# Projections of a graph network's first attention: score factors stored once and doubled by the loads, the first attention loads issued ahead of the meeting, 30 of 157 row sums placed behind the products

## The chip, the core and the metric

One core of a Trainium2 chip (trn2) runs the whole kernel. The metric is the device time of one execution in microseconds (us). The engines named below: TensorE (PE in the rows; PEld is its loading of weights), VectorE (DVE), ScalarE (ACT), GpSimd (POOL) and SyncE (SP), which here only issues DMAs. They run side by side and meet at semaphores.

## The reference, cut to what matters

Four layers of a graph network on 3125 nodes with 96 features and 100000 edges, sorted by destination. The change touches the first and, through the row sums, the last:

```python
h = relu(layernorm(x))
q = (h[src] @ qW).reshape(e, 4, 24);  k = (h[dst] @ kW).reshape(e, 4, 24);  v = (h[dst] @ vW)...
exp_s = exp(clip(einsum('ehd,ehd->eh', q, k), -10, 10))
w = exp_s / (segment_sum(exp_s, src)[src] + 1e-08)
x = x + h + segment_sum(w * v, src)
# layers 2 and 3: gated messages, neighbour sums
deg = segment_sum(ones, src);  dis = where(deg > 0, rsqrt(max(deg, 1)), 0)   # layer 4
```

## The kernel before

The kernel first builds CT, the matrix of edge counts between nodes, in SBUF (25 tiles of 128 rows, 3136 columns, float16). Everything later works on CT, and three meetings of all five engines (`meet`, L71) separate four stages: build, projections, attention, and propagation with the last layer.

**Projections.** The nodes are taken in seven blocks of 512 (the last has 64). For each block b TensorE turns the normalised features (`turn`, L868), multiplies them with the query and key weights (`products`, L896) and with the value weights (L902). The score factors must be more exact than float16, so each is kept as a high part (ScalarE, `highs`, L831) and a low part (VectorE, `low`, L783) in `K.QH[:, b % 2]`, two slots in turn. SP stores them (`proj_sync`, L675) to HBM buffers `qd` and `kd` of 4 x 24 rows for each of four heads: qd holds high, high, low, low and kd holds high, low, high, low, so that one product over 96 rows gives all four cross terms. Each part is stored twice through a broadcast, four transfers of 192 KB a block. `highs(b)` waits for the four stores of block b - 2 before it overwrites their slot. SP then waits for all stores, meets, and only then issues the first attention loads.

**Attention.** It runs over 175 iterations: seven blocks of source nodes b (512 columns in blocks 0 to 3, 384 in 4 and 5, 320 in 6), and for each 25 tiles t of destinations. In an iteration TensorE computes four scores (L1065) from Kb and Qb, ScalarE their exponentials (L1117), GpSimd clamps them (L978), TensorE turns the counts (L1054), VectorE weighs (L1136), and TensorE multiplies with the values (L1075), in that order per iteration: scores of it + 2, counts of it + 1, values of it - 1. SP issues K loads (L1012) into a ring of NK = 3 slots: the load for it + 3 waits for the scores of it. At t = 0 of blocks 1 to 5 it issues the Q load (L1005) of the next block, at t = 5 it waits for VectorE's sum of the block before and stores it (L1023), at t = 10 it loads the next x1 (L1018). All on the one queue of SP, in this order.

**Propagation.** TensorE works through seven groups of nodes: it turns and multiplies them (`linear`, L1281 and L1290), adds one eighth of the row sums of CT (`source_sums`, L1307, 157 matmuls of up to 500 columns into one bank) and starts the first product (L1299), while VectorE normalises and splits the groups (L1464 to L1516). After the last group VectorE reduces the bank to the source degrees (`degrees`, L1439).

The lines printed below are those of the kernel before.

Of the kernel before, what the change touches and what calls it, by code (L numbers as in the profile page):

```python
# [651 lines left out]
def proj_sync(q, K):  # L652
# [19 lines left out]
    def store(to, b, n, i):  # L672

        wb = width(b)
        q.dma_start(to.rearrange("r c h w -> (c h) r w")[:, :, 0:wb], bcast_out(K.QH[:, b % 2, n, i, 0:wb], 2, wb)  # L675
                    ).then_inc(S("q_out%d" % (b % 2)), 16)

    for b in range(7):
        q.wait_ge(S("q_low"), 2 * b + 1)
        for i in range(2):  # L680
            store(K.qd[b, 2 * i:2 * i + 2], b, 0, i)
        q.wait_ge(S("q_low"), 2 * b + 2)
        for i in range(2):
# [126 lines left out]
def proj_scalar(a, K):  # L810
# [47 lines left out]
def proj_tensor(t, K):  # L858
    S, bank = K.S, K.bank

    def turn(b):
# [5 lines left out]
        for i in range(tiles(b)):  # L867
            m = t.transpose(bank((0, 3)[b % 2])[0:96, 128 * i:128 * i + 128], K.hb[:, 4 * b + i, :], K.identf[:, :])  # L868
# [73 lines left out]
def alloc_attn(K, st):  # L942
# [5 lines left out]
    K.Qb = sb(st, "Qb", [96, 2, 4, 512], F16)  # L948
    K.Kb = sb(st, "Kb", [96, NK, 4, 128], F16)
# [17 lines left out]
def q_loaded(b):  # L967
    return 16 * sum(len(list(q_pieces(i))) for i in range(b % 2, b + 1, 2))
# [27 lines left out]

def attn_sync(q, K):
    S = K.S

    def q_load(b):  # L1000
        if b >= 2:
            q.wait_ge(S("scores"), 2 * (25 * (b - 2) + 24) + 2)
        for c, w in q_pieces(b):
            o = c - 128 * B0[b]
            q.dma_start(K.Qb[:, b % 2, :, o:o + w], K.qd[c // 512].rearrange("r c h w -> (r c) h w")[:, :, c % 512:c % 512 + w]  # L1005
                        ).then_inc(S("q_in%d" % (b % 2)), 16)

    def k_load(it):
        b, t, wb, na, r = dims(it)
        if it >= NK:  # L1010
            q.wait_ge(S("scores"), 2 * (it - NK) + 2)
        q.dma_start(K.Kb[:, it % NK, :, 0:r], K.kd[t // 4].rearrange("r c h w -> (r c) h w")[:, :, 128 * (t % 4):128 * (t % 4) + r]  # L1012
                    ).then_inc(S("k_in%d" % (it % NK)), 16)
# [30 lines left out]
def attn_tensor(p, K):  # L1044
# [13 lines left out]
    def score(it, k):  # L1058
# [3 lines left out]
        p.wait_ge(S("k_in%d" % (it % NK)), 16 * (it // NK + 1))  # L1062
# [114 lines left out]
SRC_W = 20  # L1177
SRC_N = (NP + SRC_W - 1) // SRC_W
# [95 lines left out]
def prop_tensor(p, K):  # L1274
# [29 lines left out]
    def source_sums(i):  # L1304
        for k in range(i * SRC_N // 8, (i + 1) * SRC_N // 8):
            w = min(SRC_W, NP - SRC_W * k)
            m = p.matmul(bank(FIRST - 1)[:, 0:NT * SRC_W].rearrange("p (a w) -> p a w", w=SRC_W)[:, :, 0:w], K.identb[:, :],  # L1307
                         K.CT[:, :, SRC_W * k:SRC_W * k + w], start=(k == 0), stop=(k == SRC_N - 1), skip_group_check=True)
# [120 lines left out]
def prop_vector(v, K):  # L1429
# [428 lines left out]
def gnn_kernel(nc, x, srcp, dstp, ewp, qW, kW, vW, Wv, bv, W2, b2, w2, bb2, w3, bb3, w4, bb4,  # L1858
               attn_w, attn_b, fus_w, fus_b, gamma, beta, out):
    with ExitStack() as ctx:  # L1860
# [10 lines left out]
        K.qd, K.kd = dram("qd", 7, 4, 24, 4, 512, dt=F16), dram("kd", 7, 4, 24, 4, 512, dt=F16)  # L1871
# [112 lines left out]
```

## Time and profile before

| | us |
|---|---|
| median of 3 runs (1189.02 to 1191.69) | 1190.76 |
| the profiled execution | 1189.85 |
| its span on the core | 1187.9 |
| busy TensorE, VectorE | 1017.8 (86%), 888.2 (75%) |
| busy ScalarE, GpSimd | 605.4 (51%), 488.9 (41%) |
| projections, from the first to the second meeting | 361 to 409.6 |
| attention, to the third meeting | 409.6 to 794.6 |

The span is what the profiled instructions cover; the time of an execution is 1.9 us longer. Times inside the profile count from the span's start. 77% of the chain that ended last is TensorE's.

### The profile page before, as it was taken

To read this page: it belongs to the slowest core of one execution; us is meant where nothing else is said; L and a number is where in the kernel's file an instruction comes from. 1 tells how busy PE (TensorE), PEld (TensorE's weight loads), DVE (VectorE), ACT (ScalarE), POOL (GpSimd) and SP (SyncE) were. 2 spreads that over 40 slices of the span, in tenths; PEclk is the share of its full clock that TensorE was granted. 3 is DMA by queue.
4 is the path that set the end of the run, shared out by engine and by line. 5 is a ranking of instruction groups with operands and counts; after the bars stand their busy time and mean duration, and the time that the engine had idled before them with its cause. 6 is when DMAs were issued, how large, how long until landed. Compare 5 with 4: busy or idle time off the path is not lost.

```text
span 1187.9 us, 23158 instructions
## 1 busy us (share of the span) xinstructions
PE 1017.8 (86%) x8352; PEld 623.3 (52%) x8352; DVE 888.2 (75%) x1338; ACT 605.4 (51%) x816; POOL 488.9 (41%) x518
## 2 busy tenths in 40 slices
PE   3887777778879599999999999987997899998983
PEld 2554555445545322222233333334587799998873
DVE  8768887888665489999999999978656464533576
ACT  7556556555653399898989898851000000000321
POOL 8545433532100089999999999840000000000000
PEclk9879888887788889999999999988999799999996
DMA  0010000000001811212122222220000000010201
GB/s 8 27 42 10 5 6 5 6 9 6 15 1 48 247 41 43 68 42 69 43 66 45 70 58 66 67 69 1 1 28 34 25 35 10 2 40 8 84 17 41
DMA packets 98906, 44.79 MB, mean 38 GB/s; under 512 B 85196, under 2 KB 96716, under 8 KB 98672
## 3 DMA queue, kind: packets, MB, share of 16 engines
q1 hardware_dynamic: 97104, 41.58, 13.2%
q0 software_dynamic: 1696, 1.74, 0.5%
q8 instruction: 74, 1.21, 0.4%
q14 instruction: 32, 0.26, 0.1%
HBM read 30.73 MB, written 12.56 MB: 36 GB/s over the span
## 4 chain that ended last, share of the span: by engine, by line
PE 77%; issue 8%; DVE 7%; ACT 3%; POOL 3%; DMA 2%; SPq 1%; DVEq 0%; ACTq 0%; POOLq 0%
PE PS L1299 17%; PE PS L1065 12%; PE PS L553 11%; PE PS L1075 11%; PE PS L557 8%; PE PS L1739 3%; PE PS L1307 3%; PE PS L1054 3%; ACT Eb L1117 2%; PE PS L1290 1%; POOL Eb L978 1%; DVE Eb L1136 1%; PE PS L878 1%; PE PS L1746 1%; PE PS L1729 1%
## 5 line engine op out<-in xcount | busy, mean ns | idle before, releaser
L1136 DVE TENSOR_TENSOR Eb<-Eb,PS 128x2048 f32<-128x2048 f32 (+4 forms) x175 | 342.1, 2014 | 20.8 <-POOL Eb L978 10.6
L1117 ACT ACTIVATE Eb<-PS,small 128x1024 f32<-128x1024 f32 (+4 forms) x350 | 333.6, 1004 | 37.2 <-PE PS L1065 32.3
L978 POOL TENSOR_SCALAR Eb<-Eb 128x1024 f32<-128x1024 f32 (+4 forms) x350 | 318.9, 935 | 79.1 <-ACT Eb L1117 75.3
L593 ACT ACTIVATE CT<-PS 128x500 f32 x313 | 183.8, 587 | 143.4 <-PE PS L557 135.6
L553 PE MATMUL PS<-mov,oneS 128*128 128x100 f16 x1565 | 185.3, 232 | 76.8 <-issue 71.7
L553 PEld LDWEIGHTS PS<-mov,oneS 128*128 128x128 f16 x1565 | 147.1, 108 | 159.6 <-issue 114.6
L1299 PE MATMUL PS<-hs,CT 128*128 128x192 f16 (+1 forms) x2500 | 213.4, 247 | 3.6 <-DVE SG L1540 1.6
L1299 PEld LDWEIGHTS PS<-hs,CT 128*128 128x128 f16 (+1 forms) x2500 | 208.0, 99 | 7.3 <-DVE SG L1540 2.3
L1065 PE MATMUL PS<-Qb,Kb 96*128 96x512 f16 (+3 forms) x700 | 180.8, 362 | 14.5 <-DMA Kb<-kd 10.2
L435 DVE TENSOR_TENSOR oneS<-iotaX,KL 128x2560 f16<-128x2560 int16 x80 | 120.5, 1506 | 72.2 <-PE PS L557 69.6
L1075 PE MATMUL PS<-Eb,V 128*25 128x512 f32 (+3 forms) x1400 | 166.9, 549 | 0.8 <-DVE Eb L1136 0.8
L1065 PEld LDWEIGHTS PS<-Qb,Kb 96*128 96x128 f16 (+1 forms) x700 | 42.4, 98 | 199.6 <-ACT Eb L1117 185.7
L557 PE MATMUL PS<-CT,identb 128*128 x313 | 144.2, 461 | 0.9 <-ACT CT L593 0.8
L435 DVE TENSOR_TENSOR mov<-iotaM,KL 128x2000 f16<-128x2000 int16 x80 | 98.0, 1225 | 0.0
L217 POOL TENSOR_SCALAR key<-hi 120x128 f32<-120x128 int32 x14 | 8.8, 628 | 173.2 <-DVE hi L444 173.1
L1054 PEld LDWEIGHTS PS<-identb,CT 128*128 128x128 f16 (+1 forms) x625 | 49.6, 99 | 44.4 <-DVE Eb L1136 8.0
L1420 ACT ACTIVATE hs<-PS 96x96 f32<-96x96 f32 x9 | 2.2, 247 | 138.3 <-PE PS L1331 138.3
L1054 PE MATMUL PS<-identb,CT 128*128 128x128 f16 (+1 forms) x625 | 66.7, 220 | 4.4 <-DVE Eb L1136 4.4
L1540 DVE TENSOR_REDUCE SG<-PS 128x96 f32<-128x192 f32 (+1 forms) x75 | 24.8, 353 | 60.7 <-PE PS L1299 60.3
L1739 PE MATMUL PS<-hs,CT 97*128 97x297 f32 (+1 forms) x200 | 44.4, 366 | 0.0
L1307 PE MATMUL PS<-CT,identb 128*128 128x500 f16 (+1 forms) x157 | 39.1, 407 | 3.3 <-SPq L71 3.3
L1739 PEld LDWEIGHTS PS<-hs,CT 97*128 97x128 f32 (+1 forms) x200 | 36.2, 196 | 6.9 <-issue 0.6
(273 smaller groups left out, 892.4 us busy)
## 6 DMA issues: line engine op xcount, KB each, us to landing
Kb<-kd SPq DMA_DIRECT2D x168, 96.0 KB, 2.3
qd<-QH SPq DMA_DIRECT2D x12, 192.0 KB, 3.0
kd<-QH SPq DMA_DIRECT2D x12, 192.0 KB, 3.2
hs<-t_d SPq DMA_DIRECT2D x12, 192.0 KB, 2.6
Qb<-qd SPq DMA_DIRECT2D x4, 384.0 KB, 3.6
CT<-x_d SPq DMA_DIRECT2D x1, 1200.0 KB, 9.2
x_d<-B SPq DMA_DIRECT2D x6, 192.0 KB, 1.8
t_d<-A SPq DMA_DIRECT2D x6, 192.0 KB, 1.8
```

What stands on the lines that cost most here:

```text
L435: return v.tensor_tensor(out.rearrange("p e (c two) -> p e c two", two=2), v_in, k_in, ALU.is_equal)
L553: t.matmul(to, K.oneS[:, s % DEEP, o + k, :], K.mov[:, s % DEEP, o + k, :].rearrange("p (a w) -> p a w", a=25), start=(k == 0), stop=False ...
L557: t.matmul(ps, K.identb[:, :], K.CT[:, :, bass.ds(vals[0], GI * W)], start=False, stop=True, skip_group_check=True).then_inc(S("counted"), 1)
L593: a.activation(K.CT[:, :, bass.ds(words[g % 4][0], GI * W)], K.bank(g % 4)[:, 0:25 * GI * W].rearrange("p (a c) -> p a c", a=25), ACT.Copy ...
L978: g.tensor_scalar(e, e, EHI, ELO, ALU.min, ALU.max).then_inc(S("clamped"), 1)
L1054: m = p.transpose(K.cntv[it % 2][0:r, 128 * i:128 * i + w], K.CT[0:w, B0[b] + i, 128 * t:128 * t + r], K.identb[0:w, 0:w])
L1065: m = p.matmul(bank(h)[0:r, 0:wb], K.Kb[:, it % NK, h, 0:r], K.Qb[:, b % 2, h, 0:wb], start=True, stop=True)
L1075: m = p.matmul(bank(4)[32 * h:32 * h + 25, 0:wb], K.V[0:r, t, h, :], K.Eb[0:r, it % NE_, h, 0:wb], start=(t == 0), stop=(t == NT - 1), til ...
L1117: a.activation(e, ps, ACT.Exp, scale=K.unsc[0:r, :]).then_inc(S("score_exp"), 1)
L1136: v.tensor_tensor(e, e, cn, ALU.mult).then_inc(S("weighed"), 1)
L1299: m = p.matmul(bank(t % FIRST)[0:r, 0:w], K.CT[:, a, 128 * t:128 * t + r], hs[:, a, :, :].rearrange("p k d -> p (k d)"), start=(a == 0), s ...
L1739: m = p.matmul(ps[:, c:297], K.TT[0:r, s, 128 * k:128 * k + 128], K.GC[0:r, k, c:297], start=(k == 0), stop=(k == 3), skip_group_check=True)
```

## The change

- `qd` and `kd` hold two parts instead of four rows of parts, high and low once each: one store per factor and block, without the broadcast (14 stores instead of 28).
- The doubling moves to the loads. A Q load is four transfers of 24 partitions, each part read twice; a K load is two of 48 partitions, the same source twice.
- SP issues the loads of Q blocks 0 and 1 and of the first three K tiles before the second meeting, behind waits for the stores that they read. `Qb` and `Kb` are therefore allocated beside the projection buffers, and `hb` becomes a ring of 16 tiles with a wait for the turns of the block that used it.
- The first 30 of the 157 row-sum matmuls run after the last products, into bank 0; VectorE reduces them into `K.part`. The other 127 stay in the eight places between the groups of propagation, and `degrees` adds the two sums.

The diff, cut to its core:

```diff
@@ -607,12 +607,30 @@
+SRC_W = 20
+SRC_N = (NP + SRC_W - 1) // SRC_W
+EARLY = 30
+
+def row_sums(p, K, b, i, j):
+    for k in range(i, j):
+        w = min(SRC_W, NP - SRC_W * k)
+        m = p.matmul(K.bank(b)[:, 0:NT * SRC_W].rearrange("p (a w) -> p a w", w=SRC_W)[:, :, 0:w], K.identb[:, :],
+                     K.CT[:, :, SRC_W * k:SRC_W * k + w], start=(k in (0, EARLY)), stop=(k in (EARLY - 1, SRC_N - 1)),
+                     skip_group_check=True)
+    return m
+
+def add_rows(v, K, b, out):
+    return v.tensor_reduce(out, K.bank(b)[:, 0:NT * SRC_W].rearrange("p (a w) -> p a w", w=SRC_W), AX.X, ALU.add)
-    K.hb = sb(st, "hb", [128, NT, D], F32)
+    K.hb = sb(st, "hb", [128, 16, D], F32)
@@ -669,26 +687,29 @@
-        q.dma_start(to.rearrange("r c h w -> (c h) r w")[:, :, 0:wb], bcast_out(K.QH[:, b % 2, n, i, 0:wb], 2, wb)
+        q.dma_start(to.rearrange("i c h w -> (c h) i w")[:, :, 0:wb], K.QH[:, b % 2, n, :, 0:wb]
                     ).then_inc(S("q_out%d" % (b % 2)), 16)
 
     for b in range(7):
         q.wait_ge(S("q_low"), 2 * b + 1)
-        for i in range(2):
-            store(K.qd[b, 2 * i:2 * i + 2], b, 0, i)
+        store(K.qd[b], b, 0)
         q.wait_ge(S("q_low"), 2 * b + 2)
-        for i in range(2):
-            store(K.kd[b, i:4:2], b, 1, i)
+        store(K.kd[b], b, 1)
...
+    q.wait_ge(S("q_out0"), 32 * 3)
+    q_load(q, K, 0)
+    for it in range(NK):
+        k_load(q, K, it)
+    q.wait_ge(S("q_out1"), 32 * 3)
+    q_load(q, K, 1)
+    q.wait_ge(S("q_out0"), 32 * 4)
     q.wait_ge(S("x1_out"), 32)
-    q.wait_ge(S("q_out0"), 64 * 4)
-    q.wait_ge(S("q_out1"), 64 * 3)
@@ -719,11 +740,14 @@
+        if b >= 4:
+            v.wait_ge(S("h_turned"), b - 3)
@@ -802,6 +826,8 @@
+    v.wait_ge(S("src_part"), 1)
+    add_rows(v, K, 0, K.part).then_inc(step, own.up())
@@ -827,7 +853,7 @@
-                a.wait_ge(S("q_out%d" % (b % 2)), 64 * (b // 2))
+                a.wait_ge(S("q_out%d" % (b % 2)), 32 * (b // 2))
@@ -927,7 +953,9 @@
+    row_sums(t, K, 0, 0, EARLY).then_inc(S("src_part"), 1)
     t.wait_ge(S("v_made"), 7)
+    t.wait_ge(S("src_part"), 1)
@@ -994,23 +1020,29 @@
+def q_load(q, K, b):
+    S = K.S
+    if b >= 2:
+        q.wait_ge(S("scores"), 2 * (25 * (b - 2) + 24) + 2)
+    for c, w in q_pieces(b):
+        o = c - 128 * B0[b]
+        for r in range(4):
+            q.dma_start(K.Qb[24 * r:24 * r + 24, b % 2, :, o:o + w], K.qd[c // 512, r // 2, :, :, c % 512:c % 512 + w]
+                        ).then_inc(S("q_in%d" % (b % 2)), 16)
+
+def k_load(q, K, it):
+    S = K.S
+    b, t, wb, na, r = dims(it)
+    if it >= NK:
+        q.wait_ge(S("scores"), 2 * (it - NK) + 2)
+    kt = K.kd[t // 4].rearrange("i c h w -> (i c) h w")[:, :, 128 * (t % 4):128 * (t % 4) + r]
+    for i in range(2):
+        q.dma_start(K.Kb[48 * i:48 * i + 48, it % NK, :, 0:r], kt).then_inc(S("k_in%d" % (it % NK)), 16)
@@ -1023,16 +1055,12 @@
-    q_load(0)
-    for it in range(NK):
-        k_load(it)
-    q_load(1)
     x1_in(0)
@@ -1302,10 +1328,7 @@
+        m = row_sums(p, K, FIRST - 1, EARLY + i * (SRC_N - EARLY) // 8, EARLY + (i + 1) * (SRC_N - EARLY) // 8)
@@ -1436,9 +1459,10 @@
+        add_rows(v, K, FIRST - 1, K.degs).then_inc(S("src_kept"), 1)
         v.wait_ge(S("src_kept"), 1)
+        v.tensor_tensor(K.degs, K.degs, K.part, ALU.add).then_inc(step, own.up())
+        v.wait_ge(step, own.n)
@@ -1868,7 +1892,7 @@
-        K.qd, K.kd = dram("qd", 7, 4, 24, 4, 512, dt=F16), dram("kd", 7, 4, 24, 4, 512, dt=F16)
+        K.qd, K.kd = dram("qd", 7, 2, 24, 4, 512, dt=F16), dram("kd", 7, 2, 24, 4, 512, dt=F16)
```

What stands in a row on the engines now, in the three places that matter. On TensorE at the end of the projections (L896 and L922 are the factor products, L902 and L928 the value products, L1065 and L1093 the first scores), before:

```order
L902 MATMUL PS<-wv,hTb 128x96 x4
L868 MATMUL PS<-identf,hb 96x128
L896 MATMUL PS<-hTb,wqk 96x512 x2
L902 MATMUL PS<-wv,hTb 128x96 x4
L896 MATMUL PS<-hTb,wqk 96x64 x2
L902 MATMUL PS<-wv,hTb 64x96
L1065 MATMUL PS<-Qb,Kb 128x512 x8
```

and after the change:

```order
L928 MATMUL PS<-wv,hTb 128x96 x4
L894 MATMUL PS<-identf,hb 96x128
L922 MATMUL PS<-hTb,wqk 96x512 x2
L928 MATMUL PS<-wv,hTb 128x96 x4
L922 MATMUL PS<-hTb,wqk 96x64 x2
L928 MATMUL PS<-wv,hTb 64x96
L619 MATMUL PS<-CT,identb 128x500 x30
L1093 MATMUL PS<-Qb,Kb 128x512 x8
```

The row sums (L619) stand between the last value product and the meeting that precedes the first scores.

On SP in the same place, the stores of the last two blocks and the first loads; before, the meeting stands behind the last store:

```order
L688 DMA x_d<-X 128x1248
L675 DMA qd<-QH 96x2x512 x2
L675 DMA kd<-QH 96x2x512 x2
L675 DMA qd<-QH 96x2x64 x2
L675 DMA kd<-QH 96x2x64 x2
L1005 DMA Qb<-qd 96x2048
L1012 DMA Kb<-kd 96x4x128 x3
L1005 DMA Qb<-qd 96x2048
L1018 DMA xb<-x_d 128x384
```

and after the change, with the meeting behind the last of the 14 loads:

```order
L704 DMA x_d<-X 128x1248
L693 DMA qd<-QH 96x2x512
L693 DMA kd<-QH 96x2x512
L693 DMA qd<-QH 96x2x64
L693 DMA kd<-QH 96x2x64
L1030 DMA Qb<-qd 24x2048 x4
L1041 DMA Kb<-kd 48x4x128 x6
L1030 DMA Qb<-qd 24x2048 x4
L1050 DMA xb<-x_d 128x384
```

Eight stores have become four, five loads have become fourteen, and these have moved ahead of the meeting.

On SP at the start of attention block 4, where the two pieces of Q for block 5 are loaded between K loads; before:

```order
L1012 DMA Kb<-kd 96x4x64
L1012 DMA Kb<-kd 96x4x128 x4
L1005 DMA Qb<-qd 96x4x128
L1005 DMA Qb<-qd 96x4x256
L1012 DMA Kb<-kd 96x4x128 x5
```

and after the change:

```order
L1041 DMA Kb<-kd 48x4x64 x2
L1041 DMA Kb<-kd 48x4x128 x8
L1030 DMA Qb<-qd 24x4x128 x4
L1030 DMA Qb<-qd 24x4x256 x4
L1041 DMA Kb<-kd 48x4x128 x10
```

The K load behind the Q loads has eight issues ahead of it instead of two, and is itself two.

## Rows read from the trace of the kernel before

**Rows 1.** Chain of waits, 400 to 414 us: start, us, what.

```profile
401.11 3.27 DMA kd<-QH
...
407.98 1.60 DMA kd<-QH
...
410.02 3.50 DMA Kb<-kd
...
413.91 1.03 PE PS L1065 x2
```

**Rows 2.** Waits of ScalarE, 380 to 410 us: total us, times, longest.

```profile
ACT QH L831 <- DMA kd<-QH: 8.0, 5, 2.5
```

**Rows 3.** Timeline of TensorE, end of the products: start us, us, operation.

```profile
400.91 0.48 PE L896 MATMUL PS<-hTb,wqk 96*96 96x64 f32 x4
```

**Rows 4.** Timeline of ScalarE and VectorE, last block and the second meeting.

```profile
404.46 0.33 ACT L831 ACTIVATE QH<-PS 96x64 f16<-96x64 f32 x2 [1.21 <-DMA kd<-QH]
...
404.72 0.35 DVE L783 TENSOR_TENSOR QH<-PS,QH 96x64 f16<-96x64 f32 x2 [1.01 <-ACT QH L831]
...
410.91 0.08 DVE L1128 MEMSET rs<- 128x25 f32 x1
```

**Rows 5.** Windows: us, busy PE, PEld, DVE, ACT, POOL, then PEclk, DMA share, GB/s.

```profile
390.00:401.00 11.00, 10.47 (x57) 6.67 (x56) 7.42 (x19) 5.46 (x12) 0.00 (x0) 1.00 0.92 284
...
405.00:410.00 5.00, 0.00 (x0) 0.00 (x0) 0.30 (x2) 0.00 (x0) 0.00 (x0) 0.50 0.67 185
...
807.00:808.00 1.00, 0.00 (x0) 0.00 (x0) 0.97 (x5) 0.04 (x1) 0.00 (x0) 0.66 0.00 0
```

**Rows 6.** Timeline of SP: issues of K and Q loads in blocks 4 and 5.

```profile
650.95 0.54 SPq L1012 DMA_DIRECT2D Kb<-kd  x1
651.53 1.28 SPq L1005 DMA_DIRECT2D Qb<-qd  x2
...
665.89 1.86 SPq L1012 DMA_DIRECT2D Kb<-kd  x3
...
698.53 0.54 SPq L1012 DMA_DIRECT2D Kb<-kd  x1
```

**Rows 7.** Lines L675, L1005 and L1012: duration of an issue, ns min/median/max; landing.

```profile
L675 SPq DMA_DIRECT2D qd<-QH x14: 304/467/1352, 386.7 to 406.8; - x14
...
L1005 SPq DMA_DIRECT2D Qb<-qd x9: 315/617/618, 409.7 to 699.8; - x9
...
L1012 SPq DMA_DIRECT2D Kb<-kd x175: 540/541/659, 410.0 to 781.0; - x175
...
DMA to landing us min/median/max: 2.1/2.3/3.5
```

**Rows 8.** Timeline of TensorE: the starts of four scores in blocks 4 and 5.

```profile
657.80 0.87 PE L1065 MATMUL PS<-Qb,Kb 96*128 96x384 f16 x3
...
668.27 0.82 PE L1065 MATMUL PS<-Qb,Kb 96*128 96x384 f16 x4
...
703.15 0.97 PE L1065 MATMUL PS<-Qb,Kb 96*128 96x384 f16 x4
...
705.00 0.78 PE L1065 MATMUL PS<-Qb,Kb 96*128 96x384 f16 x3
```

**Rows 9.** Chain of waits, 828 to 834 us: row sums at full clock.

```profile
829.45 4.33 PE PS L1307 x20
```

**Rows 10.** Timeline of TensorE, 794 to 804 us: first row sums and products.

```profile
794.69 7.06 PE L1307 MATMUL PS<-CT,identb 128*128 128x500 f16 x19 [3.28 <-SPq L71]
...
803.09 1.13 PE L1290 MATMUL PS<-WL,hs 97*128 97x96 f32 x8 [0.68 <-ACT hs L1395]
```

**Rows 11.** Waits in propagation: VectorE 812 to 862, TensorE 794 to 862.

```profile
DVE TR L1513 <- PE PS L1290: 2.8, 3, 1.0
...
PE PS L1281 <- DVE SG L1479: 4.2, 1, 4.2
```

**Rows 12.** Timeline of VectorE, the reduction of the row sums.

```profile
862.98 0.68 DVE L1439 TENSOR_REDUCE small<-PS 128x25 f32<-128x500 f32 x1 [7.44 <-PE PS L1307]
```

More of the change, by code:

```diff
@@ L670, in proj_sync, with store @@
     q.dma_start(K.WL[96:97, 1, :], K.b2.rearrange("(o d) -> o d", o=1)).then_inc(S("wl_in"), 16)
-    def store(to, b, n, i):
+    def store(to, b, n):
         wb = width(b)
-        q.dma_start(to.rearrange("r c h w -> (c h) r w")[:, :, 0:wb], bcast_out(K.QH[:, b % 2, n, i, 0:wb], 2, wb)
+        q.dma_start(to.rearrange("i c h w -> (c h) i w")[:, :, 0:wb], K.QH[:, b % 2, n, :, 0:wb]
                     ).then_inc(S("q_out%d" % (b % 2)), 16)
@@ L721, in norm @@
         sl = slice(4 * b, 4 * b + tiles(b))
+        ring = slice(4 * (b % 4), 4 * (b % 4) + tiles(b))
+        if b >= 4:
+            v.wait_ge(S("h_turned"), b - 3)
         for t in range(4 * b, 4 * b + tiles(b)):
-            c = v.tensor_scalar(K.hb[:, t, :], K.X[:, t, :], K.mv[:, t, 0:1], K.rs[:, 2, t:t + 1], ALU.subtract, ALU.mult)
+            c = v.tensor_scalar(K.hb[:, t % 16, :], K.X[:, t, :], K.mv[:, t, 0:1], K.rs[:, 2, t:t + 1], ALU.subtract, ALU.mult)
         c.then_inc(S("h0"), 1)
         v.wait_ge(S("h0"), b + 1)
-        v.scalar_tensor_tensor(out=K.X[:, sl, :], in0=K.hb[:, sl, :], scalar=0.0, in1=K.X[:, sl, :], op0=ALU.max, op1=ALU.add
+        v.scalar_tensor_tensor(out=K.X[:, sl, :], in0=K.hb[:, ring, :], scalar=0.0, in1=K.X[:, sl, :], op0=ALU.max, op1=ALU.add
                                ).then_inc(S("x1"), 1)
@@ L867, in turn @@
         for i in range(tiles(b)):
-            m = t.transpose(bank((0, 3)[b % 2])[0:96, 128 * i:128 * i + 128], K.hb[:, 4 * b + i, :], K.identf[:, :])
+            m = t.transpose(bank((0, 3)[b % 2])[0:96, 128 * i:128 * i + 128], K.hb[:, 4 * (b % 4) + i, :], K.identf[:, :])
         m.then_inc(S("h_turned"), 1)
@@ L967, in q_loaded @@
 def q_loaded(b):
-    return 16 * sum(len(list(q_pieces(i))) for i in range(b % 2, b + 1, 2))
+    return 64 * sum(len(list(q_pieces(i))) for i in range(b % 2, b + 1, 2))
 def attn_gpsimd(g, K):
@@ L994, in gamma @@
                          ).then_inc(K.S("gamma_in%d" % i), 16)
+def q_load(q, K, b):
[15 more added lines that the diff above has]
+        q.dma_start(K.Kb[48 * i:48 * i + 48, it % NK, :, 0:r], kt).then_inc(S("k_in%d" % (it % NK)), 16)
 def attn_sync(q, K):
     S = K.S
[L1000 to L1013, printed above, removed]
     def x1_in(b):
@@ L1032, in attn_sync @@
         if it + NK < len(ITS):
-            k_load(it + NK)
+            k_load(q, K, it + NK)
         if t == 0 and 0 < b < 6:
-            q_load(b + 1)
+            q_load(q, K, b + 1)
         if t == 5 and b:
@@ L1061, in score @@
             p.wait_ge(S("score_exp"), 2 * (it - 1) + k + 1)
[L1062 removed]
+        p.wait_ge(S("k_in%d" % (it % NK)), 32 * (it // NK + 1))
         p.wait_ge(S("q_in%d" % (b % 2)), q_loaded(b))
@@ L1304, in source_sums @@
     def source_sums(i):
[L1305 to L1308, printed above, removed]
+        m = row_sums(p, K, FIRST - 1, EARLY + i * (SRC_N - EARLY) // 8, EARLY + (i + 1) * (SRC_N - EARLY) // 8)
         if i == 7:
@@ L1886, in gnn_kernel @@
         K.mv = K.sb(ctx, "mv", [128, NT, 2], F32)
+        K.part = K.bns[:, 16:21, :].rearrange("p t s -> p (t s)")[:, 0:NT]
         K.WL = K.sb(ctx, "WL", [97, 2, D], F32)
@@ L1891, in gnn_kernel @@
             K.V = K.sb(stv, "V", [128, NT, 4, 25], F32)
+            K.Qb = K.sb(stv, "Qb", [96, 2, 4, 512], F16)
+            K.Kb = K.sb(stv, "Kb", [96, NK, 4, 128], F16)
             with ExitStack() as st:
```

6 lines of the change are left out of this document (removed).

## The prediction, made before the change ran

> **What bounds the kernel now.** I read the chain of waits first, then the timeline around the two meetings, then the waits of the engines there. Most of the span is TensorE's own work; what the change touches is three places.
>
> The end of the projections (386 to 414 us). QH, the SBUF copy of the score factors, has two slots; ScalarE may write a slot only when the stores of the block before last have landed. Each block stores 768 KB in four transfers. ScalarE waited 8.0 us in five pieces for such a store [rows 2], and the last stores land at 409.58, which releases the meeting [rows 1]. Behind it come the first loads: K lands at 413.52, and the first score starts at 413.91. TensorE had finished the products of the last block at 401.39 [rows 3]. So between 401.4 and 413.9 the path is transfers only.
>
> The attention loop. Its front is TensorE and ScalarE in alternation; SP loads K three iterations ahead, so a K load normally has slack. I set each K landing against the start of the score that reads it: in blocks 4 to 6 the load issued after SP's wait for the x1 sum leaves almost none. It is issued at 665.89 and lands 2.3 us later, at 668.2 [rows 6, 7]; its score starts at 668.27 [rows 8]. An ordinary one, issued at 698.53, has landed at 700.8, and its score starts at 703.15: 2.3 us of slack.
>
> Propagation (794 to 863 us). The row sums stand between the groups of the first product, 157 matmuls. VectorE is nearly full there: from 812 to 862 it waited for TensorE 2.8 us in all [rows 11].
>
> **The change part by part.**
>
> Stores. 28 of 192 KB become 14, 384 KB a block. A store lands some 3 us after its issue (401.11 to 404.38 today [rows 1]); the next use of its slot is two blocks on, some 6 us, so I take ScalarE's waits for the stores as gone. What is late next is TensorE's own stream, which sets 401.39 already now [rows 3]. From there: the high part on ScalarE 0.33 and the low part on VectorE 0.35 for the 64 columns [rows 4], and two issues of 0.47: SP has issued its last store at 402.6 instead of about 408. The range is 402.2 to 403.5.
>
> Loads ahead of the meeting. SP now issues 14 loads where it issued 5 after the meeting: 4 of 24 partitions for Q, 6 of 48 partitions for K, 4 for the second Q. They are not free: the meeting waits until SP has issued them. No row shows such a form. The nearest: 0.467, the median of a store to qd, 0.541 for a K load of 96 partitions, 0.617 for a Q load [rows 7]; the lowest issue is 0.304, a store behind an idle queue. I take 0.47 for Q, the median, and 0.54 for K, as now, gaps included, 7.0 us in all; the bounds are 14 x 0.35 = 4.9 and 14 x 0.66 = 9.2, the lowest and the Q load's with a gap of 0.04. So SP meets at 402.6 + 7.0 = 409.6, between 407.5 and 411.8. The loads themselves land while SP still issues, so the 3.5 us of the K load [rows 1] leave the path.
>
> Row sums behind the products. 30 matmuls of 500 columns on TensorE. At full clock 20 take 4.33 us, 0.2165 each [rows 9]: 6.5 us. The granted clock is 1.00 from 390 to 401 with TensorE 95% busy [rows 5], and the sums follow with hardly a gap (the values product of the last block lies between, 0.4), so I take the full clock. They end at 408.3, the VectorE sum of 0.68 [rows 12] at 409.0. That is just below SP's 409.6: the sums are hidden, with 0.6 us of cover.
>
> After the meeting VectorE's three memsets set the first score: released at 409.58, the last ends at 410.99 [rows 4], 1.4 us. First score 411.0 instead of 413.9: **-2.9 us**; with SP at its bounds -3.5 (then VectorE's 409.0 ends last) and -0.7.
>
> Clock at the start of attention. Before, TensorE was at half clock from 405 on [rows 5], and its first scores ran at it: two in 1.03 us [rows 1]. Now it idles from 408.3 to 411.0, 2.7 us. The nearest row: it worked until 804.22 [rows 10], and the clock fell within 807 to 808 (0.66 there [rows 5]). A tie; a full clock would give 0.5 on the first two scores and by my estimate about 1 more on the scores, counts and value products of the first four iterations. I take **-0.6**, range 0 to -1.6.
>
> K loads in pairs, Q loads in fours. Bytes are the same; each K load needs two issues, so its second half starts about 0.5 later (bounds 0.35 and 0.58). Where the slack is 1.8 or more that costs nothing: the work that hides it is two iterations of scores. Behind the x1 sum the slack is 0.1 in blocks 4 to 6; blocks 1 to 3, with 512 columns and slower iterations, have more and pay nothing. The Q loads are queued ahead of a K load: in blocks 4 and 5 they were two issues (651.53, 1.28 us [rows 6]) and are eight, 3.8 us. K there: 650.95 + 0.95 (a pair) + 3.8 = 655.7, plus 0.5 and 2.3 to land, 658.5, where the score starts at 657.80 [rows 8]: 0.7 late. Block 5: 698.53 + 0.95 + 3.8 + 0.5 + 2.3 = 706.0 against 705.00: 1.0 late. Blocks 1 to 3 have four issues and slower iterations: not late. The front goes 1.85 us an iteration there (703.15 to 705.00 [rows 8]) and the others follow it, so its stall is lost in full. The x1 sum comes later by a part of it only, so the load behind that sum adds little in blocks 4 and 5, by my estimate 0.1 and 0.2, and its whole 0.5 in block 6. Together **+2.5 us**, between 0.3 (issues of 0.35) and 5.5 (issues of 0.62).
>
> Propagation. 127 row sums instead of 157: at most 30 x 0.2165 = 6.5 us. The first chunk, 19 matmuls at mostly half clock in 7.06 us [rows 10], ended as VectorE's first group was ready, and TensorE waited 4.2 us before the second [rows 11]: four matmuls fewer give nothing. In chunks two to six VectorE becomes the bound; what TensorE gives it is exactly its 2.8 us of waiting [rows 11]. The last two chunks come after VectorE has run out of work and are on the path: 8 matmuls, 1.7 us. The added VectorE sum (0.2) stands behind the reduction that frees the bank, so TensorE does not wait for it. **-4.5 us**, between -1.7 and -6.5.
>
> The ring of hb (16 tiles instead of 25) adds a wait for a turn three blocks back, long done; the move of Qb and Kb in SBUF costs nothing.
>
> Here the Trainium skill speaks against the change. No row shows a load of 24 partitions. The page DMA: Bandwidth & Descriptors (section Why a DMA increments its semaphore by 16 and not by 1) says that a transfer is spread over the largest number of engines, up to 16, that divides its slowest dimension: a 24-partition load would use 12 of 16. Its Rules for kernel authors add that transfers to disjoint partition parts are not worth splitting, since they share the engines. By that the Q data loaded in block 4 (96 x 384 columns x 4 heads, 288 KB, 1.0 us at the 284 GB/s of [rows 5]) would take 1.35, and K behind it in blocks 4 and 5 would be 0.3 later each: the sum 0.6 us worse.
>
> **The sum.** -2.9 - 0.6 + 2.5 - 4.5 = -5.5 us. The profiled execution took 1189.85 (span 1187.9), so 1184.35; the median of the runs lies 0.9 above it: **1185.3**. A measurement of this kernel tells 0.2%, 2.4 us, from no change.
>
> **The rivals.**
>
> SP as the bound (the other side). If an issue costs u instead of 0.48, the 14 before the meeting, the 16 in the two Q bursts and the late K pairs cost 33 x (u - 0.48). From u = 0.65 the gain is gone; at 0.80 it is +10.6 - 5.5 = +5.1, 1195.8. For it: a store took up to 1.352 [rows 7]. Against: that came with 284 GB/s in flight [rows 5], which the halved stores no longer make; at 0.617 throughout it is still -1.0, 1189.8.
>
> Row sums at half clock. At half clock a matmul takes twice its 0.2165, 30 take 13.0 us, end at 414.8, and the first score is at 417.0 instead of 411.0: +6.0, the sum +0.5, 1191.3. Against it: the clock is full right before.
>
> VectorE hides the propagation gain. Only the two last chunks count, -1.7 instead of -4.5: 1188.1. Against it: the 2.8 us are waits that a row shows.
>
> Split Q loads that move at three quarters of the rate, so that K behind them is 0.3 us later twice: 1185.9.
>
> All goes better: SP issues small loads at 0.36, no late K, the clock stays: -3.5 - 1.6 + 0.3 - 5 = -9.8, 1181.0.
>
> **How the numbers follow.** Forecast, with the narrow-engine case (1182.5 to 1188.2) 0.68; SP at 0.58 to 0.65 (1188.4 to 1190.8) 0.12; half clock 0.08; slower through SP (over 1193) 0.05; better than 1182 0.07. Faster by over 0.2%, that is under 1188.4: 0.77; the same 0.17; slower 0.06. The range 1181.5 to 1190.5 leaves out some 0.07 below and 0.07 above.
>
> **What would show it.** Right: ScalarE has no wait for a store over 0.3 us; 14 load issues between 402.6 and about 409.6; the 30 matmuls in 6.5 us ending ahead of SP's meeting; first score at about 411; in blocks 4 and 5 a K load landing 0.5 to 1 us behind its score's turn; VectorE without waits for TensorE in the middle chunks of row sums, and its reduction of the degrees 4.5 us nearer to the stage's start. Wrong: issues of the small loads near 0.3 or above 0.65, row sums at 0.42, or a stage of propagation shortened by less than 3 us.

## The result, and the profile after

The change made the kernel slower by 0.55%: 1196.43 us median (1192.62 to 1201.33, 12 runs) against 1190.03 (1185.74 to 1191.69, 12 runs), ratio 1.0055, interval 1.0037 to 1.0074. The forecast was 1185.3, the range ended at 1190.5. The profiled execution of after is the slowest of its twelve (1201.33, span 1199.60), so its difference of 11.65 us in the span is read as where the time goes, and its size against the median's 6.4 is taken up below.

The stages, from the starts of the first transpose of h, of the scores of an iteration, and the end, in the timelines of TensorE:

| stretch, us | before | after | difference |
|---|---|---|---|
| start to the first transpose of h (untouched) | 379.32 | 380.62 | +1.30 |
| to the first score | 34.60 | 32.74 | -1.86 |
| iterations 0 to 25 | 59.79 | 60.63 | +0.84 |
| 25 to 100 (blocks 1 to 3) | 176.40 | 176.39 | 0 |
| 100 to 125 (block 4) | 47.58 | 53.39 | +5.81 |
| 125 to 150 (block 5) | 47.11 | 52.94 | +5.83 |
| 150 to 174 (block 6) | 40.31 | 44.69 | +4.38 |
| last score to the end | 402.85 | 398.21 | -4.64 |

The first row is no work of the change: from 42.4 to 44.6 us TensorE had the clock 1.00 before and 0.50 after, in the same code. Of the rest, start and propagation went the way that the prediction said, iterations 0 to 25 went the other way, and blocks 4 to 6 took 16 us more. SP's timeline where block 4 starts (start us, us, operation), the one that answers to [rows 6]:

```profile
651.25 1.19 SPq L1041 DMA_DIRECT2D Kb<-kd  x2
652.48 6.77 SPq L1030 DMA_DIRECT2D Qb<-qd  x8
659.29 1.87 SPq L1041 DMA_DIRECT2D Kb<-kd  x3
```

Eight Q issues take 6.77 us where two took 1.28, and the K load behind them is issued at 659.29, before at 653.04. It lands at 662.09. The scores that wait for it, in TensorE's timeline, against 657.80 before [rows 8]:

```profile
656.35 0.83 PE L1093 MATMUL PS<-Qb,Kb 96*128 96x384 f16 x4
662.18 1.44 PE L1093 MATMUL PS<-Qb,Kb 96*128 96x384 f16 x4 [4.01 <-issue]
665.30 1.46 PE L1093 MATMUL PS<-Qb,Kb 96*128 96x384 f16 x4
669.00 0.81 PE L1093 MATMUL PS<-Qb,Kb 96*128 96x384 f16 x4
```

These scores start 4.4 us later than before (0.3 of it brought along), and two iterations on the front is 7.0 us behind (669.00 against 661.96). The windows of the same stretch (columns as in [rows 5]) show why:

```profile
656.00:660.00 4.00, 2.17 (x19) 0.66 (x15) 4.00 (x4) 2.32 (x3) 3.94 (x5) 1.00 0.17 44
660.00:662.00 2.00, 0.00 (x0) 0.00 (x0) 0.50 (x1) 0.00 (x0) 0.00 (x0) 0.95 0.31 76
662.00:664.00 2.00, 1.82 (x11) 0.96 (x15) 0.02 (x1) 0.98 (x2) 0.00 (x0) 0.50 0.34 77
...
666.00:668.00 2.00, 2.00 (x14) 0.65 (x12) 0.88 (x1) 1.69 (x2) 0.86 (x2) 0.50 0.02 6
668.00:670.00 2.00, 2.00 (x19) 1.19 (x19) 1.60 (x4) 0.48 (x1) 0.76 (x1) 0.84 0.22 49
```

TensorE stands still for 4 us, the granted clock falls to 0.50 at 661.8, and the next 6.4 us run at that level (1.2 GHz): a set of four scores takes 1.44 us instead of 0.83. Of the 7.0 us, 4.4 are there when the late load lands and the rest comes at the low clock; about 1 comes back after it. The start of block 5 repeats it: eight issues from 706.31, the next K at 712.82, TensorE idle for 4.7 us, the clock at 0.50 from 713.0 to 719.8.

The lines of the loads (duration ns min/median/max, answering to [rows 7]):

```profile
L1030 SPq DMA_DIRECT2D Qb<-qd x36: 360/757/1105, 404.4 to 712.0; - x36
...
L1041 SPq DMA_DIRECT2D Kb<-kd x350: 537/602/1626, 406.1 to 797.9; - x175
```

The end of the projections, SP's timeline:

```profile
403.91 0.45 SPq L693 DMA_DIRECT2D kd<-QH  x1
404.40 1.64 SPq L1030 DMA_DIRECT2D Qb<-qd  x4
406.08 3.89 SPq L1041 DMA_DIRECT2D Kb<-kd  x6
410.02 1.77 SPq L1030 DMA_DIRECT2D Qb<-qd  x4
```

and TensorE's, the row sums, with ScalarE's one remaining wait for a store in the list of waits (8.0 us before [rows 2]):

```profile
402.47 6.66 PE L619 MATMUL PS<-CT,identb 128*128 128x500 f16 x30
```

```profile
ACT QH L857 <- DMA kd<-QH: 0.9, 1, 0.9
```

### The profile page after: what moved, and what is told of

It is laid out like the page before. It is cut to its first block, busy times and chain, and to the rows that moved or that the text cites. A ratio compares the mean times of both kernels' runs of the same rounds, so it can differ in the third digit from the quotient of the medians.

```text
span 1199.6 us, 23347 instructions
## 1 busy us (share of the span) xinstructions
PE 1025.8 (86%) x8352; PEld 626.7 (52%) x8352; DVE 890.1 (74%) x1340; ACT 606.3 (51%) x816; POOL 487.5 (41%) x518
## 4 chain that ended last, share of the span: by engine, by line
PE 75%; issue 9%; DVE 9%; ACT 3%; POOL 2%; DMA 1%; SPq 1%; DVEq 0%; ACTq 0%; POOLq 0%
PE PS L1325 17%; PE PS L1093 12%; PE PS L553 11%; PE PS L1103 11%; PE PS L557 8%; PE PS L1763 3%; PE PS L1082 3%; ACT Eb L1145 2%; PE PS L619 1%; PE PS L1316 1%; PE PS L904 1%; PE PS L1770 1%; PE PS L1753 1%; POOL Eb L1004 1%; DVE Eb L1164 1%
## 5 line engine op out<-in xcount | busy, mean ns | idle before, releaser
L1093 PE MATMUL PS<-Qb,Kb 96*128 96x512 f16 (+3 forms) x700 | 183.6, 369 | 19.1 <-issue 10.6
L1103 PE MATMUL PS<-Eb,V 128*25 128x512 f32 (+3 forms) x1400 | 170.8, 561 | 1.0 <-DVE Eb L1164 1.0
L1093 PEld LDWEIGHTS PS<-Qb,Kb 96*128 96x128 f16 (+1 forms) x700 | 43.6, 99 | 207.7 <-ACT Eb L1145 183.6
L619 PE MATMUL PS<-CT,identb 128*128 128x500 f16 (+1 forms) x157 | 39.5, 409 | 3.3 <-SPq L71 3.3
```

The source lines that it names most:

```text
L1093: m = p.matmul(bank(h)[0:r, 0:wb], K.Kb[:, it % NK, h, 0:r], K.Qb[:, b % 2, h, 0:wb], start=True, stop=True)
L1103: m = p.matmul(bank(4)[32 * h:32 * h + 25, 0:wb], K.V[0:r, t, h, :], K.Eb[0:r, it % NE_, h, 0:wb], start=(t == 0), stop=(t == NT - 1), til ...
```

## The experiments

Each ran beside the kernel before on the same chip; ratios are to it. The runs stand in four groups on four chips, e1 to e4, e5 to e8, e9 to e12 and e13, so a difference between two groups is less certain than one inside a group. Theory A is my reading of the trace: the loss is SP's issue time, in the bursts of Q loads and, less, in the K pairs.

**Merged loads: e1, e2, e3.** Fewer issues for the same doubled data, by a source that repeats itself.

```
-    for i in range(2):
-        q.dma_start(K.Kb[48 * i:48 * i + 48, it % NK, :, 0:r], kt)...
+    q.dma_start(K.Kb[:, it % NK, :, 0:r], kt.unsqueeze(0).to_broadcast([2, 48, 4, r]))...
...
-        for r in range(4):
-            q.dma_start(K.Qb[24 * r:24 * r + 24, ...], K.qd[c // 512, r // 2, ...])...
+        for i in range(2):
+            q.dma_start(K.Qb[48 * i:48 * i + 48, ...], src.unsqueeze(0).to_broadcast([2, 24, 4, w]))...
```

> The changed kernel with its loads merged: each K load is one transfer to 96 partitions whose source repeats the stored factors (one issue where the change has two), each Q piece two transfers to 48 partitions (two issues where it has four). Stores once, early loads and early row sums stay. Theory A (SyncE's issue time is the loss: 8 narrow Q issues of 0.76 us and K pairs of 1.28 us in place of 0.54): a K load lands some 2.3 us after its issue again, the attention loop runs as in the kernel before (scores 0 to 174 in 371 us against 371.2 before and 388.0 in the changed kernel), the first score comes at 411 to 412, and the propagation's 4.5 us stay: about 1184 us. Theory B (the transfers, which read one stored copy twice, are what is late, however they are issued): landing stays 2.8 us and over behind the issue and blocks 4 to 6 still lose several us: 1188 or more.

> The changed kernel, only Q's loads merged to two transfers of 48 partitions a piece; K stays in pairs. Theory A: 4 narrow issues of 0.62 to 0.76 us in place of 8 of 0.76 at the start of blocks 4 and 5 give SyncE back 3.0 to 3.8 us there, so of the 5.8 and 6.0 us lost in these blocks some 2 stay in each, and block 6, which has K pairs alone, still loses 3 to 4: 1188 to 1190 us. Theory B (late transfers): the blocks lose what they lost, 1195 to 1197.

> The changed kernel, only K's loads merged to one transfer; Q stays in four transfers a piece. Theory A: the burst of 8 narrow Q issues (6.4 us) still delays the fifth K load of blocks 4 and 5 by 5 us, of which a slack of 2.3 us swallows a part: 2.8 us lost in each; block 6 loses nothing. 1186 to 1188 us. If the pairs of K alone were the cause, 1184; if the Q bursts alone were, 1192 or more.

Measured: e1 (both) 1342.04 us, ratio 1.1288 (1.1264 to 1.1312); e3 (K alone) 1315.22, 1.1056 (1.1033 to 1.1079); e2 (Q alone) 1214.23, 1.0214 (1.0194 to 1.0234). Every expectation missed: neither theory had this in it. The line of e3's K loads, and a window of 5 us of these transfers:

```profile
L1040 SPq DMA_DIRECT2D Kb<-kd x175: 615/2434/2929, 406.5 to 909.5; - x175
```

```profile
503.00:508.00 5.00, 4.51 (x36) 1.97 (x36) 4.90 (x6) 3.79 (x4) 4.76 (x5) 1.00 0.18 41
```

One issue of the repeated source takes 2.43 us where two plain ones take 1.2. Its packets of 256 B follow each other evenly at 141 per us, 26 to 30 in each 0.2 us of that window; a K load of before moves its 384 packets in 0.8 us, up to 227 in 0.2 us. So the transfer itself is slow, 41 GB/s in the window. SP is held up behind it: the first issue after a pause took 0.64 us (at 507.48), the one right behind it 2.31. The Trainium skill, DMA: Bandwidth & Descriptors (section Why a DMA increments its semaphore by 16 and not by 1), says that a transfer uses the largest number of engines, up to 16, that divides the slowest dimension of both sides; here that dimension is the repeat of 2. The trace is near to that and no proof of it: the DMA share of 0.18 is 2.9 of 16 engines, and the trace does not name the engines. These runs replaced one cost with another, so they decide nothing on theory A.

**The row sums alone: e4.** The kernel before with only the move of the 30 row sums.

```
     # kernel before, end of the products on TensorE
+    row_sums(t, K, 0, 0, EARLY).then_inc(S("src_part"), 1)
     t.wait_ge(S("v_made"), 7)
+    t.wait_ge(S("src_part"), 1)
```

> The kernel before with only the row sums moved: 30 behind the products, 127 in the propagation; stores and loads as before. Theory A: attention starts where it did (first score 413.9 less up to 0.6 for a faster clock), the propagation is 4.5 us shorter: about 1185.5 us. Rival C (the TensorE clock gives the gain back, the mean granted clock having fallen from 0.922 to 0.914 in the changed kernel): 1188 or more.

Measured: 1189.68 us (1183.28 to 1192.41, 12 runs), ratio 0.9999 (0.9981 to 1.0017): no gain. From the last score to the end it took 398.43 us, 4.4 less than before, as theory A said. It was paid at the other end: from the first transpose to the first score 37.87 us, 3.3 more. TensorE's timeline and the windows:

```profile
401.95 0.58 PE L922 MATMUL PS<-wv,hTb 96*64 96x96 f32 x2 [1.20 <-ACT V L856]
402.46 7.99 PE L619 MATMUL PS<-CT,identb 128*128 128x500 f16 x30
```

```profile
401.90:404.00 2.10, 2.05 (x6) 0.87 (x7) 0.45 (x1) 0.16 (x2) 0.00 (x0) 0.50 1.04 362
404.00:406.00 2.00, 2.00 (x8) 0.78 (x7) 0.35 (x2) 0.30 (x3) 0.00 (x0) 0.69 0.95 309
```

ScalarE still waits for the stores there, TensorE idles for it (1.20 us, and more before), the clock is at 0.50 when the sums begin, they end at 410.45, and the first load goes at 411.35 (before 409.7 [rows 7]). The total is rival C's, but the gain of the propagation stays whole. What eats it lies ahead of it: the 3.3 us of the start, which neither side had named, 1.1 in iterations 0 to 25, and in this execution 1.3 in block 6. So alone, behind stores that still hold up ScalarE, the early sums pay nothing, and the half clock that the prediction had as a rival does come there, for a part of them: 7.99 us, where the changed kernel took 6.66.

**Spreading the Q loads, and moving a wait: e5, e6.** The same transfers as the change, other places.

```
-        if t == 0 and 0 < b < 6:
-            q_load(q, K, b + 1)
-        if t == 5 and b:
+        if 0 < b < 6 and t % 3 == 0:
+            q_load(q, K, b + 1, q_parts(b + 1)[t // 3:t // 3 + 1])
+        if t == 8 and b:                      # e6 alone; e5 keeps t == 5
             x1_back(b - 1)
```

> The changed kernel, the same transfers, but the Q loads of the next block are issued one at a time, every third iteration of the block, in place of all at its start. Theory A (SyncE's issue time in a burst): 6.4 us of issues in a row no longer stand ahead of the fifth K load; blocks 4 and 5 lose under 1 us each in place of 5.8 and 6.0, block 6, which has no Q load, still loses 3 to 4 with its K pairs behind the wait for the sum of x1: 1185 to 1188 us. Rival D (the sum of SyncE's work is too much for an iteration of 1.8 us, wherever it is issued): a pair and a Q issue take 2.0 us, and the blocks lose 2 us and more each: 1189 to 1193.

> As the run with the Q loads spread, and in addition the store of the block's sum of x1, for which SyncE waits behind the K load of iteration 8, is issued at iteration 8 of the block in place of iteration 5, so that the K loads of iterations 9 to 11 are issued before that wait. Theory A: the K load of iteration 9 has its normal slack, and what blocks 1 to 6 lose there goes, above all block 6's 3 to 4 us: 1182 to 1185 us. If the refill behind the wait costs nothing once the Q bursts are gone: no difference from the run with the loads spread alone.

Measured: e5 1187.74 us, ratio 0.9968 (0.9949 to 0.9986); e6 1182.25, 0.9916 (0.99 to 0.9931). Both totals lie where theory A put them; block 4 of e5 lost 1.1 us, where it said under 1. Nothing but the place of the Q issues differs between the changed kernel and e5, and in the traces block 4 takes 48.69 us instead of 53.39, block 5 47.95 instead of 52.94. Block 6, which loads no Q, keeps its loss (43.43 us, before 40.31) until e6 takes the wait for the x1 sum out of the way of the K pairs (40.20). Windows of block 6, e5 and then e6:

```profile
762.00:764.00 2.00, 0.26 (x5) 0.13 (x2) 1.80 (x2) 0.49 (x1) 1.29 (x2) 0.96 0.32 69
764.00:766.00 2.00, 2.00 (x15) 0.87 (x14) 0.46 (x1) 1.37 (x2) 0.50 (x1) 0.50 0.25 56
```

```profile
762.00:764.00 2.00, 2.00 (x25) 0.78 (x17) 1.92 (x2) 1.74 (x3) 1.66 (x3) 1.00 0.48 123
764.00:766.00 2.00, 1.99 (x19) 0.79 (x18) 1.75 (x2) 1.70 (x3) 1.84 (x4) 1.00 0.33 74
```

**Four copies again, in whole or for Q: e7, e8.**

```
-        store(K.qd[b], b, 0)
+        for i in range(2):
+            store_twice(K.qd[b, 2 * i:2 * i + 2], b, 0, i)     # and each Q piece one load
...
-        store(K.kd[b], b, 1)                                   # e7 alone
+        for i in range(2):
+            store_twice(K.kd[b, i:4:2], b, 1, i)               # and each K load one transfer
```

> The changed kernel with the stores and loads of the kernel before (28 stores, each Q piece and each K load one transfer); the loads ahead of the meeting and the early row sums stay. Theory A: the attention loop runs as before (371.2 us from the first score to the last), ScalarE waits again for the stores, so the row sums end at 410 to 410.5 and the meeting is at 411.4, the first score at 412.5 to 413; the clock rises some 1 us later (as in the run with the sums alone), the propagation is 4.4 us shorter: 1185.5 to 1187.5. If the split loads were not the loss: 1193 and more.

> The changed kernel with qd stored four times again and each Q piece one transfer; kd is stored once and each K load is a pair. Theory A: the pairs' share of the loss alone. Two Q issues (1.3 us) at the start of blocks 4 and 5, K landing 2.8 us after its issue: under 1 us lost there, some 0.5 to 1 behind the wait for the sum of x1 in blocks 4 and 5, 3 in block 6; start and propagation gain some 5: 1188 to 1190 us. If the Q burst were the whole loss: 1184 to 1186.

Measured: e7 1187.91 us, ratio 0.9974 (0.9958 to 0.999), 0.4 over its expectation; e8 1184.29, 0.9942 (0.9926 to 0.9959). That is under theory A's 1188 and inside the range of the other reading, that the Q burst is the whole loss. e8's six executions fall in two groups, four from 1182.83 to 1184.49 and two at 1188.1 and 1188.21, and the profile is of the slowest. With whole Q loads and K pairs, blocks 4 and 5 take 48.17 and 47.13 us, against 47.58 and 47.11: the pairs alone cost 0.6 us there, the Q bursts all the rest. In e8's profile block 6 still loses 2.9 us; that the four fast executions are without this loss would fit their times, but no profile shows one. e7 has no split load at all; its blocks 4 and 5 take 47.71 and 47.48. Its start misses the expectation (35.30 us to the first score): ScalarE waits 8.0 us for stores as before, the row sums run 7.91 us partly at half clock to 411, and their reduction on VectorE ends last, at 411.67.

**What the rest is worth: e9 to e12.** e9 and e10 are e6 with the second block's Q loads, or all 14 first loads, behind the meeting; e12 is e6 with 1 early row sum instead of 30; e11 is the kernel before with the x1 store at iteration 8.

```
-    q.wait_ge(S("q_out1"), 32 * 3)
-    q_load(q, K, 1)
+    q.wait_ge(S("q_out1"), 32 * 3)
...
     x1_in(0)
+    q_load(q, K, 1)                                            # e9
```

> As e6_spread_back, but the Q loads of the second block (4 issues, 1.66 us) go behind the meeting, behind the load of xb. SyncE is the last at the meeting in e6 (410.56; the row sums' reduction ends at 408.1), so the meeting is at 408.7 and the first score 1.85 us earlier: 1180.4 us, and up to 1 us less if the first products still run at the full clock. If something else (the landing of the K load, VectorE) held the first score: 1182.

> As e6_spread_back, but all of the first 14 loads go behind the meeting, as in the kernel before. The reduction of the early row sums ends last, at 408.1; Q's four and K's first two issues take 2.9 us from there, the landing 2.1: first score at 413.2 against 412.08 in e6, 1183.3 us or up to 1.5 us more for a clock that rises later. If the early loads are worth what the prediction gave them and the 3.5 us of landing were all gained: 1185.

> The kernel before with nothing changed but the store of a block's sum of x1, issued at iteration 8 in place of 5. In its trace the K load of iteration 9 lands 0.09 us before its score in blocks 4 to 6, but blocks 4 to 6 take as long as in e6 to 0.2 us. Theory A (it matters only where the K loads are pairs): 1190 us, no change. If the wait costs the kernel before as well: 1187 to 1188.

> As e6_spread_back, but 1 row sum behind the products and 156 in the propagation in place of 30 and 127. Theory A: the propagation's gain goes (4.3 us), and attention starts when it did, since SyncE, not TensorE, ended the stage; its first products run at half clock for longer, 0 to 1 us: 1186.5 to 1187.5. Rival C (what the sums give is taken back by the clock or the start, as with the sums alone, where the total gained 0.1): 1182 to 1183.5.

Measured: e9 **1178.93** us (1176.51 to 1181.8), 0.9906 (0.989 to 0.9922), faster than both kernels; e10 1182.65, 0.9937 (0.9922 to 0.9951); e11 1190.62, 1.0 (0.9987 to 1.0012); e12 1187.49, 0.9977 (0.9967 to 0.9988). All as theory A expected, e9 and e10 1.5 and 0.6 us under its number. The early row sums are worth 5.2 us once the stores are halved, by the medians of e12 and e6; those are of two groups, and by the ratios it is 7.3. In the two traces the propagation accounts for 4.8 of it (398.31 us from the last score to the end, against 403.11); the first score comes 1.0 later in e6, and a clock that rose sooner gives it 1.9. The x1 store's place is worth nothing without the pairs. The first loads ahead of the meeting, in the form the change gave them, are worth little, since SP issues them while everyone waits: e10 against e6, again of two groups, is 0.4 us by the medians and 2.5 by ratios whose intervals overlap. With the four that nobody needs yet behind the meeting it is 3.7 us (e10 against e9, of one group). In e9 VectorE's reduction of the sums ends the stage, not SP:

```profile
404.77 0.68 DVE L627 TENSOR_REDUCE bns<-PS 128x25 f32<-128x500 f32 x1 [6.41 <-PE PS L619]
```

```profile
401.20 3.89 SPq L1043 DMA_DIRECT2D Kb<-kd  x6
```

**The price of a form: e13.** The changed kernel, narrow Q loads cut in other ways, still in bursts.

```
+def q_forms(b):
+    n, m = {3: (24, 2), 4: (24, 1), 5: (24, 2), 6: (12, 4)}.get(b, (24, 4))     # partitions, heads
+    return [(r, p, n, h, m) for r in range(4) for p in range(0, 24, n) for h in range(0, 4, m)]
```

> The changed kernel with the narrow Q loads cut in other forms, all still in one burst: block 4 as 24 partitions with 1 head each (16 issues of 24 runs), block 5 as 24 with 2 heads (16 issues of 48 runs), block 6 as 12 with 4 heads (16 issues of 48 runs); block 3, whole pieces, as 24 with 2 heads. If the number of runs set the price: about 0.36 for 24 runs, 0.5 for 48. If it is the partitions and not the runs: 0.76 for 24 partitions whatever the heads, another value for 12. If 24 partitions with more than one run is the costly form: 0.36 for block 4 and 0.76 for block 5. In any case the kernel is slower than the changed one by the issues added in bursts: 1200 to 1220 us.

Measured: 1208.01 us in 2 runs, ratio 1.0155 (1.0104 to 1.0206). The bursts for block 5 (24 partitions, 2 heads) and block 6 (12 partitions, 4 heads) in SP's timeline:

```profile
651.48 7.69 SPq L1035 DMA_DIRECT2D Qb<-qd  x16
```

```profile
705.73 12.81 SPq L1035 DMA_DIRECT2D Qb<-qd  x16
```

12.81 / 16 is 0.80 with the gap of 0.04; 7.69 / 16 is 0.48, but one of the sixteen took 1.300 and the first 0.56, the others 0.37; with 1 head (block 4) it was 0.365. Both forms have 48 runs. So neither the number of runs nor that of the partitions sets the price by itself: 1 or 2 heads cost 0.37 at 24 partitions, 4 heads 0.76 at 24 partitions as at 12. None of my three guesses holds. Why 48 or 96 partitions with 4 heads cost less (0.60 and 0.62) stays open, and it did not matter for the verdict: two issues at 0.37 are as long as one at 0.76.

## Why the prediction was wrong, step by step

**Stores.** Right in the main. ScalarE's waits went from 8.0 to 0.9 us; the prediction had them gone, with none over 0.3. SP was through its last store at 404.36, forecast 402.6: 1.3 of that are the first row of the table, 0.5 the stage's own.

**Loads ahead of the meeting.** Right in size: the 14 issues took 7.39 us from 404.40 to 411.79 (forecast 7.0, and SP the last at the meeting). The parts were not: with their gaps a Q issue took 0.43 instead of 0.47, a K issue 0.66 instead of 0.54.

**Row sums.** Right: 6.66 us at a clock of 1.00, hidden, forecast 6.5. e4 and e7, with all the stores of before, took 7.99 and 7.91, partly at half clock; that the full clock hangs on the shorter waits for stores the prediction didn't say.

**First score.** 1.86 us earlier (in its own stage), forecast 2.9. Of the 1.0 missing, 0.5 is the last store, 0.4 the issues, 0.2 the way from the meeting to the score.

**Clock at the start of attention.** Wrong sign, and outside the range of 0 to -1.6, though the prediction had called it a tie: TensorE idled 4.2 us, not 2.7, because SP came later. The clock fell at 412.6, ahead of the first score, and was back only 12.9 us behind that score, before the change 11.1. Iterations 0 to 25 took 0.84 more, not 0.6 less. The windows of before and then of after:

```profile
424.00:426.00 2.00, 2.00 (x15) 0.60 (x14) 2.00 (x2) 1.21 (x2) 1.80 (x3) 0.74 0.21 48
```

```profile
424.00:426.00 2.00, 2.00 (x9) 0.17 (x6) 2.00 (x1) 0.66 (x1) 1.78 (x2) 0.50 0.22 49
426.00:428.00 2.00, 2.00 (x16) 0.70 (x14) 0.98 (x2) 1.38 (x2) 0.18 (x1) 0.93 0.00 0
```

e6 idled longer still (4.7 us) and had the full clock back 8.7 us behind its first score, e9 idled 2.4 and waited 13.6 for it: iterations 0 to 25 took 58.88 and 60.96 us. So a shorter idle time alone does not bring the clock back sooner; e6's 2 us are luck as far as these runs tell.

**K in pairs, Q in fours. This is the step that failed.** The term said "they were two issues ... and are eight, 3.8 us", 0.47 each, +2.5 in all. The eight took 6.77. The number came from the stores to qd, of which no one has the form of a narrow piece. The whole pieces behaved (0.36); the pieces of 64 to 384 columns, whose four heads are four runs in each partition, cost 0.757. Issues above 0.65 were among the prediction's own signs of being wrong. Put 6.77 into the prediction's own line and K lands at 661.5, 3.7 late; measured 4.4, 0.3 of it brought along.

Two further steps were missing. A stall of 4 us is not paid once: the clock falls, and a score 4 us late became 5.8 us lost per block. And block 6 lost 4.4, not 0.5. There SP refills its three K loads at 1.28 us a pair instead of 0.58 a load, so the scores behind the wait come late one after another, and the clock falls. But the pairs are not all of it: in every profile with plain loads that lost time in block 6 (the changed kernel, e4, e5, e7, e8, e13) a 16 KB packet of instructions was in flight during that refill; in e6, e9 and e10 such a packet met loads with slack, and nothing was lost. In the changed kernel the first issue behind the wait took 1.63 us, in e5 and e8 the second half of the first pair landed 3.2 and 3.3 us after its issue, where the median is 2.3. With single loads such a packet came with 1.3 us lost in e4 and 1.05 in e7. How the 4.4 divide between pairs, packet and clock stays open. With 5.8 + 5.8 + 4.4 in place of 2.5, the prediction's sum would have been +8.

The rival "SP as the bound" had the mechanism and the side; it got 0.05. Its condition (an issue over 0.65) held for the 20 narrow Q issues and 11 of the 350 K issues; the row that stood for it, a store of 1.352 amid 284 GB/s, is another form in another place. That its 1195.8 lies near the 1196.43 is luck: it is 33 issues at 0.80 without a fall of the clock. The argument against, that at 0.617 throughout nothing is lost, left out that a form no row shows has no upper bound in the rows that do.

**Propagation.** Right in mechanism, a little lucky in size: -4.64, forecast -4.5. The reduction of the degrees stands 64.35 us behind the first row sum, 3.9 nearer than before [rows 10, 12]; the other 0.7 came behind it, where the change only adds a sum of 0.2 us. Of the 3.9, 1.8 are VectorE's waits for TensorE (1.0 left of 2.8 [rows 11]) and 2.1 the wait for the last sums (5.37, before 7.44 [rows 12]). The list of VectorE's waits from 828.3 to 874.3, and its timeline:

```profile
DVE TR L1537 <- PE PS L1316: 1.0, 1, 1.0
```

```profile
875.34 0.68 DVE L627 TENSOR_REDUCE small<-PS 128x25 f32<-128x500 f32 x1 [5.37 <-PE PS L619]
```

**Narrow engines.** The rival gave K 0.3 us more behind the split Q loads. The trace shows nothing of it: the pair behind the burst of block 4 landed 2.80 us after its first issue (659.29 to 662.09), the one behind the burst of block 5 after 2.90, and the median of the pairs is 2.80. The Q issues were long themselves here; with shorter ones it stays untested.

**The median.** The sum of the profile's differences is +11.65, the medians differ by 6.4. The twelve runs of after spread over 8.7 us. The pieces that vary between profiled executions are the clock (1.3 at 42 us, 2 at the start of attention) and block 6, where e7 and e4 lost 1.05 and 1.3 at a clock of 1.00, and e8, e5 and the changed kernel 2.9 to 4.4 with it at 0.50. That the shorter executions of after are those that lost less there is argued, not shown.

## What to carry to other kernels

A queue's issue time is a resource of its own: count its issues per iteration, price each form of transfer (partitions, runs in a partition) by a row of that very form, and treat a form without a row as open upwards. A burst of issues belongs in the slack of the loop, one at a time, not ahead of the load that everyone needs next; and a wait belongs behind the loads that can go before it. Work that is moved into a gap may itself run later or at a lower clock there, so test it together with, and without, what makes the gap.

## What the hardware showed that I had not expected

**Long issues and late landings come with an instruction fetch.** Some K issues took 0.8 to 1.8 us instead of 0.6. The list of DMA queues for 770.1 to 770.4 us of the changed kernel, inside its longest K issue:

```profile
q8 instruction: 1, 0.02, 23.0%
```

```profile
770.05 1.63 SPq L1041 DMA_DIRECT2D Kb<-kd  x1
```

In eleven traces (before, after, e4 to e12) every K issue over 0.8 us, 67 in all, has a 16 KB packet of queue q8, which the profile labels instruction, in flight beside it for over 0.05 us; of the 2,830 that have none, the longest took 0.77. With single K loads 4 of 81 issues beside such a packet were stretched, both of e4's and both of e7's; with pairs 63 of 239, mostly the second of the pair. The landing can be late as well, behind an issue of ordinary length. Of the K loads issued after 430 us whose landing the same traces give, 98 of 434 with such a packet in flight took over 3 us from issue to landing, and 2 of 1,557 without. One of the 98 cost e7 its microsecond in block 6: the load issued at 758.42 in 0.54 us landed 3.4 us later, at 761.78, and the score that needs it started at 761.87 (the stretched issue of e7 at 759.7 was for a later load, which landed 2.3 us ahead of its score). Its line:

```profile
DMA to landing us min/median/max: 3.4/3.4/3.4
```

That the packet is the cause is inferred from this company; no run moved it. If it is, more issues meeting more fetches is a price of splitting transfers that no row of before could have shown: it had 21 such meetings and not one stretched issue.

**A repeated outer dimension of 2 in a transfer's source** makes it four and a half times as long to issue (e3: 2.43 us against 0.54) and cost 125 us of 1190, although no byte more is moved.

**A stall is amplified by the clock.** In the changed kernel TensorE's stalls of 4.0 and 4.7 us in the attention loop and the one of 1.7 in block 6 each came with 6.8 us at a clock of 0.50. The fall came 3.6 us into the first stall, 1.8 into the second and 0.5 behind the end of the third. In e5 and e8 a stall of 1.7 and 1.8 us came with 3.4 us at 0.50; e4's of 1.5 and e7's of 1.3 left the clock at 1.00.
